# A fused macaron block on one core: the feed-forward's residual moved from VectorE to TensorE and ScalarE, its block scales made once, its layer norm halves joined by GpSimd

## The reference

```python
def fp4_quant_dequant(x):            # blocks of 16 along the last dim
    scale = jnp.maximum(jnp.max(jnp.abs(xb), axis=-1, keepdims=True) / 6.0, 1e-12)
    xn = xb / scale
    idx = jnp.searchsorted(_MID, jnp.abs(xn))
    return (_GRID[idx] * jnp.sign(xn) * scale).reshape(shape)

def _L1_ffn_ref(x, w_gate, w_up, w_down):        # 128 -> 352 -> 128
    gate = fp4_linear(x, w_gate)                 # both operands through fp4_quant_dequant
    y = fp4_linear(x, w_up)
    h = jax.nn.silu(gate) * y
    return fp4_linear(h, w_down)

x = x + 0.5 * _L0_ffn_ref(_layernorm(x), ...)    # mixture of experts
x = x + _L0_attn_ref(_layernorm(x), ...)         # linear attention
x = x + 0.5 * _L0_ffn_ref(_layernorm(x), ...)
x = x + 0.5 * _L1_ffn_ref(_layernorm(x), ...)    # "ffn_a"
x = x + _L1_attn_ref(_layernorm(x), ...)
x = x + 0.5 * _L1_ffn_ref(_layernorm(x), ...)    # "ffn_b"
```

## Time and profile before

| | |
|---|---|
| median of 3 runs | 868.86 us |
| lowest and highest | 866.7 and 873.04 us |
| the profiled execution, its own time | 870.8 us |
| its span in the profile | 869.0 us |
| mean granted TensorE clock | 0.896 of full speed |
| PE, DVE, ACT, POOL busy | 81%, 78%, 54%, 19% of the span |
| DVE's products of gate and up (L1085) | 428.9 to 846.6 us, in both feed-forwards |

### The profile page before, as it was taken

The page is one execution under the profiler, slowest core; times in us unless marked ns, Lnnn a source line. Parts: engine busy times, 40 slices in busy tenths (PEclk is TensorE's granted clock), DMA queues, the critical chain, the costliest instruction groups (busy, mean ns, idle before and its releaser), DMA issues.

```text
span 869.0 us, 17382 instructions
## 1 busy us (share of the span) xinstructions
PE 703.0 (81%) x6018; PEld 533.8 (61%) x6018; DVE 676.8 (78%) x1671; ACT 466.8 (54%) x893; POOL 164.6 (19%) x323
## 2 busy tenths in 40 slices
PE   3999999798986999999585777468989865857774
PEld 2777776677775677776354665436686663546654
DVE  2888787375656578789799999649899956999995
ACT  3787777656460677777464455264323114644552
POOL 4001021645542100101111210022110001112100
PEclk9999999899999899999768788868999987687888
DMA  7000000000000000000000000000000000000000
GB/s 197 2 0 0 0 1 2 3 3 2 0 3 3 1 1 0 0 1 0 1 0 0 0 0 0 1 0 1 1 0 0 1 0 1 12 12 12 12 24 25
DMA packets 13454, 6.99 MB, mean 8 GB/s; under 512 B 1177, under 2 KB 13409, under 8 KB 13409
## 3 DMA queue, kind: packets, MB, share of 16 engines
q1 hardware_dynamic: 10464, 5.26, 2.3%
q10 hardware_dynamic: 2944, 1.12, 0.5%
HBM read 4.28 MB, written 2.10 MB: 7 GB/s over the span
## 4 chain that ended last, share of the span: by engine, by line
PE 60%; DVE 26%; issue 7%; ACT 3%; DMA 1%; POOL 1%; DVEq 0%; SPq 0%; POOLq 0%; ACTq 0%
PE ps L1171 53%; PE ps L1470 4%; DVE ffn_work L723 3%; DVE shared L998 2%; DVE ffn_work L728 2%; DVE picked L900 2%; PE ps L1483 2%; DVE hq L734 1%; DVE x_sb L819 1%; DVE xn L734 1%; ACT xn L435 1%; DVE ffn_work L717 1%; DVE fq_x_max L700 1%; DMA wraw<-ttn_out_proj_weight_dram 1%; DVE attT L906 1%
## 5 line engine op out<-in xcount | busy, mean ns | idle before, releaser
L1171 PEld LDWEIGHTS ps<-w_sb,sq_h 128*128 128x128 f32 x1024 | 131.9, 192 | 68.8 <-ACT sq_h L457 50.7
L819 DVE SCALAR_TENSOR_TENSOR x_sb<-ps,gates,x_sb 128x128 f32 (+1 forms) x512 | 147.8, 345 | 20.4 <-PE ps L1171 12.3
L294 POOL TENSOR_SCALAR vareps<-meanvar 128x4 f32<-128x4 f32 (+1 forms) x44 | 25.0, 568 | 606.4 <-DVEq L763 606.4
L1171 PE MATMUL ps<-w_sb,sq_h 128*128 128x128 f32 x1024 | 138.0, 278 | 0.9 <-ACT sq_h L457 0.9
L1171 PE MATMUL ps<-xnT,w_sb 128*128 128x512 f32 x256 | 135.4, 613 | 0.0
L453 ACT ACTIVATE relu_h<-ps 128x512 f32<-128x512 f32 x128 | 75.7, 591 | 57.6 <-PE ps L1171 57.3
L435 ACT ACTIVATE xn<-x_sb,shift,rstd 128x128 f32 (+1 forms) x192 | 79.8, 481 | 18.3 <-POOL shift L302 18.2
L457 ACT ACTIVATE sq_h<-relu_h 128x512 f32<-128x512 f32 x128 | 80.6, 630 | 4.0
L1483 PE MATMUL ps<-ident,xn 128*128 128x128 f32 x64 | 16.8, 414 | 70.8 <-DVE xn L734 70.8
L1171 PE MATMUL ps<-ident,shared 128*128 128x128 f32 x512 | 64.6, 290 | 10.3 <-DVE shared L998 10.3
L1171 PE MATMUL ps<-downT,hqT 128*128 128x128 f32 x384 | 71.2, 339 | 0.5 <-ACT hqT L631 0.5
(11 more groups left out here) (147 smaller groups left out, 1270.1 us busy)
## 6 DMA issues: line engine op xcount, KB each, us to landing
x_sb<-in_L_attn_x_dram SPq DMA_DIRECT2D x8, 256.0 KB, 6.4
out_dram<-x_sb SPq DMA_DIRECT2D x8, 256.0 KB, 2.3
w_sb<-in_L_ffn_w_all_dram ACTq DMA_DIRECT2D x2, 512.0 KB, 7.4
wraw<-in_L_attn_qkv_w_dram SPq DMA_DIRECT2D x1, 192.0 KB
wraw<-attn_in_proj_weight_dram SPq DMA_DIRECT2D x1, 192.0 KB
fraw<-in_L_ffn_w_down_dram SPq DMA_DIRECT2D x1, 176.0 KB, 3.5
fraw<-in_L_ffn_w_gate_dram SPq DMA_DIRECT2D x1, 128.0 KB, 4.0
fraw<-in_L_ffn_w_up_dram SPq DMA_DIRECT2D x1, 128.0 KB, 3.1
```

Of the source, the lines that this page charges most:

```text
L819: t = nc.vector.scalar_tensor_tensor(tile_b(i, j), bank(4 + e % 4, TPB, C)[:, j, :], gates[:, j, e:e + 1], tile_b(i, j), ALU.mult, ALU.add)
L1171: return nc.tensor.matmul(o, a, b, start=start, stop=stop, **kw)
```

## The change

Three things, in both feed-forwards.

**The residual.** DVE's `residual` is gone. PE multiplies `x_sb` of the group by the identity into bank 7 before the down products (`x_under`), these add on top (`start=False`), and ACT copies the bank back to `x_sb` (`x_out`). The factor 0.5 and the signs go into the weights when ACT copies them out, once.

**One scale a block.** `scales` with its two instructions is replaced by `nudged_scales` with one; the quotient and the product back use the same scale.

**The layer norm.** DVE no longer joins the two halves that the sums instruction leaves (`ln_moments` falls away for groups 2 to 7); POOL does that from the raw sums with ten small instructions in place of four (`ln_from_halves`). DVE takes the sums of group i+3 in the middle of body i, where they were those of group i+2 at its start.

```diff
+            def ln_from_halves(s, i, n):
+                half = stats[:, 0:n, :]
+                mean_sum, mean_gap, gap_sq, spread, var = [sums[:, k, 0:n] for k in range(5)]
+                base = 9 * (i - 2)
+                pool.wait_ge(s["stats_ready"], i - 1)
+                pool.sem_inc(s_passed_pool, 1)
+                k = step(0, nc.gpsimd.tensor_tensor(mean_gap, half[:, :, 1], half[:, :, 4], ALU.subtract))
+                k = step(k, nc.gpsimd.tensor_tensor(mean_sum, half[:, :, 1], half[:, :, 4], ALU.add))
+                k = step(k, nc.gpsimd.tensor_tensor(spread, half[:, :, 2], half[:, :, 5], ALU.add))
...
+                k = step(k, nc.gpsimd.tensor_tensor(rstd[:, 0:n], vareps[:, 0:n], minus_half[:, 0:n], ALU.pow))
@@ ACT
+                def x_out(i):
+                    act.wait_ge(s["down_done"], i * TPB + TPB)
+                    act.sem_inc(s_passed_act, 1)
+                    nc.scalar.activation(group_b(i), bank(7, TPB, C), ACT.Copy).then_inc(s["x_done"], 1)
@@ ACT body
                         act.wait_ge(s["tr_done"], i + 2)
                         normal(i + 2)
+                    if not (type(i) is int and i == 0):
+                        x_out(i - 1)
                     act.wait_ge(s["h_divided"], i + 1)
                     magnitude(fq_h[0], fq_h[1]).then_inc(s["h_sized"], 1)
@@ DVE
-                def residual(i):
-                    dve.wait_ge(s["down_done"], i * TPB + TPB)
-                    nc.vector.scalar_tensor_tensor(group_b(i), bank(7, TPB, C), 0.5, group_b(i),
-                                                   ALU.mult, ALU.add).then_inc(s["x_done"], 1)
+                def halves(i):
+                    for j in range(TPB):
+                        t = nc.vector.bn_stats(stats[:, j, :], tile_b(i, j))
+                    t.then_inc(s["stats_ready"], 1)
@@ DVE body
-                    if ahead:
-                        ln_stats(s, ch, i + 2, TPB, tile_b)
                     dve.wait_ge(s["up_ready"], i * TPB + TPB)
...
                     h4.largest()
-                    h4.scales()
-                    h4.inverse()
+                    h4.nudged_scales()
+                    h4.inverse(h4.sl)
                     h4.divide()
-                    if behind:
-                        residual(i - 1)
                     if ahead:
                         dve.wait_ge(s["xn_ready"], i + 3)
                         x4 = x_stream(i + 2)
                         x4.largest()
...
                         x4.divide()
+                    if further:
+                        halves(i + 3)
                     h4.snap()
@@ PE
+                def x_under(i):
+                    if not (type(i) is int and i == 0):
+                        pe.wait_ge(s["x_done"], i)
+                    mm(bank(7, TPB, C), ident[:, :], group_b(i), start=True, stop=False, skip_group_check=True)
@@ PE body
                         x_transposes(i + 2)
+                    x_under(i)
                     pe.wait_ge(s["hq_ready"], i + 1)
                     hidden_transposes(i, 0)
```

More of the change, by code:

```diff
@@ L115, in macaron @@
         shift = sb("shift", [P, 8])
+        sums = sb("sums", [P, 6, TPB])
         xn = sb("xn", [P, 8, C])
@@ L631, in hidden_T, with body @@
                     nc.scalar.activation(hqT[:, j % 2, :, :], bank(5 + j % 2, 3, P), ACT.Copy).then_inc(s["hT_ready"], 1)
-                def body(i, ahead, last):
+                def x_out(i):
+                    act.wait_ge(s["down_done"], i * TPB + TPB)
+                    act.sem_inc(s_passed_act, 1)
+                    nc.scalar.activation(group_b(i), bank(7, TPB, C), ACT.Copy).then_inc(s["x_done"], 1)
+                def body(i, ahead, last, further=False):
                     if ahead:
@@ L661, in ffn @@
                 evac_xnT(s, 1)
-                with act.Fori(0, GROUPS - 2) as i:
-                    body(i, True, False)
+                body(0, True, False, True)
+                with act.Fori(1, GROUPS - 3) as i:
+                    body(i, True, False, True)
+                body(GROUPS - 3, True, False)
                 body(GROUPS - 2, False, False)
                 body(GROUPS - 1, False, True)
+                x_out(GROUPS - 1)
             moe(S["moe_a"], S["linatt"], True)
@@ L1077, in x_alone, with body @@
                     x4.rescale()
-                def body(i, ahead, behind):
-                    if ahead:
-                        ln_stats(s, ch, i + 2, TPB, tile_b)
+                def halves(i):
+                    for j in range(TPB):
+                        t = nc.vector.bn_stats(stats[:, j, :], tile_b(i, j))
+                    t.then_inc(s["stats_ready"], 1)
+                def body(i, ahead, further):
                     dve.wait_ge(s["up_ready"], i * TPB + TPB)
@@ L1116, in ffn @@
                 x_alone(0)
+                dve.wait_ge(s["xn_ready"], 2)
+                halves(2)
                 x_alone(1)
                 pre = ch.k
[L1119 to L1123, removed]
+                with dve.Fori(0, GROUPS - 3) as i:
+                    ch.start(i * PER["ffn"] + pre)
                     body(i, True, True)
                     assert ch.k == PER["ffn"], ("ffn", ch.k)
-                pre += (GROUPS - 3) * PER["ffn"]
-                ch.start(pre)
-                body(GROUPS - 2, False, True)
-                body(GROUPS - 1, False, True)
+                ch.start((GROUPS - 3) * PER["ffn"] + pre)
+                body(GROUPS - 3, True, False)
+                body(GROUPS - 2, False, False)
+                body(GROUPS - 1, False, False)
                 if first:
@@ L1475, in down @@
                     for k in range(3):
[L1476 removed]
+                        t = mm(bank(7, TPB, C)[:, j, :], hqT[:, j % 2, k, :], downT[:, k, :], start=False, stop=k == 2,
+                               skip_group_check=True)
                     t.then_inc(s["down_done"], 1)
@@ L1501, in ffn @@
                 x_transposes(1)
-                with pe.Fori(0, GROUPS - 2) as i:
+                body(0, True, False)
+                with pe.Fori(1, GROUPS - 2) as i:
                     body(i, True, False)
```

57 lines of the change are left out of this document (42 added, 15 removed).

## The result

The changed kernel takes 880.06 us (median of 4 runs, 879.4 to 883.55) against 869.64 us (4 runs, 866.7 to 873.04): ratio 1.0131, 95% interval 1.0092 to 1.0169. It is slower by 1.3%. 886.9 was forecast, range 876 to 898: the direction and the range hold, the loss is 10.4 us where 18 were expected.

What follows compares the result with a forecast made beforehand. DVE and the chain X, PE, ACT's hidden copies, ACT's normalised x were taken to bound the kernel together. Two feed-forwards (+16.0) and POOL (+2.0) on 870.8 made 888.8; 1.9 lower for the median, 886.9 us, range 876 to 898.

Steps and rivals of the forecast that it cites:

- The bound: DVE and a chain through PE and ACT end together; 2.6 us less DVE work a body gains nothing.
- X: The moment at which DVE ends the last product on xn; one body, 17.10 us, runs between two of them.
- first stretch: From X to DVE's start on the largest of the next xn blocks: 8.35 us, not below about 8.3.
- The sums: Four sums instructions of group i+3, behind the quotient of xn, stand exposed on DVE: 0.82 us with the hand-over.
- second stretch: From DVE's start on the largest xn block to the next X: 8.75 us, forecast to become 9.47.
- The identity product: On PE ahead of the hidden transposes, 1.70 us at low clock; delays the chain 0.55 us, bounds 0.1 and 2.4.
- The copy in body 6: ACT's copy of bank 7 precedes the hidden magnitude there, so DVE waits: 2.0 us later.
- Body 7: Last body of the feed-forward: magnitude waits for DVE's quotient anyway, identity product fits PE's wait; put at -0.13 us.
- POOL: Its ten small instructions may hold DVE: 0.2 us a body, +2.0 in all.
- the count of five slips a body: Between sums and X, a small POOL instruction slips in between DVE's two-operand operations some five times, 0.04 us each.
- The sum: +8.0 us for one feed-forward, +16.0 for two, +2.0 for POOL: in all +18.
- (b): Rival: PE mostly finds the clock rising early, delay 0.15, POOL's part 0; 5.6 a feed-forward, 880 us; chance 0.22.

Runs made afterwards that it cites:

- e6: Changed kernel with identity product before xn transposes, sums before the xn wait, magnitude before bank 7's copy, ACT normalising between hidden copies: 847.57 us, ratio 0.9747.
- e2: Changed kernel with DVE taking the sums of group i+3 before it waits for ACT's xn: 872.93 us, ratio to before 1.002.
- e1: Changed kernel with PE's identity product moved ahead of the transposes of xn, inside PE's pause: 867.49 us, ratio to before 0.9949.
- e3: Changed kernel with its residual part undone (residual back on DVE, no identity product or ACT copy): 871.8 us, ratio to before 1.0019.
- e7: Kernel e3 plus a useless 128x512 product in PE's pause, ahead of the transposes of xn: 861.27 us, ratio to before 0.9906.
- e5: Changed kernel with identity product before xn transposes, sums before the xn wait, and body 6's magnitude before the copy: 856.37 us, ratio 0.9835.

## Why the prediction was right, and what was mis-sized

**The bound.** Right. The chain X, PE, hidden copies, normalised x holds the first stretch; DVE's 2.6 us less work became 2.3 to 3.5 us of waiting for L475, as stated. e6 shows it from the other side: with the normalised x taken out of that place, and the product and the sums moved, the wait is gone and the stretch is DVE's 6.5.

**The sums.** Right in size and place: second stretch 9.48 measured, 9.47 worked out. Removing that exposure (e2) gives 7.1 us.

**The identity product.** The place was right (e1), and so was its duration, 1.71 against 1.70. The delay that follows was mis-sized: the mean first stretch grew by 0.17 us, not by 0.55. This is the term of the sum that failed most, 3.8 of the 18 us forecast. The step took the middle between a rise of the clock as late as before (delay 0.9 to 1.0) and one at 3.7 us (0.1 to 0.2). Measured are distances of 3.0 to 5.7 us from the restart, and in four of the ten bodies a restart that still finds the clock up and then has it low for 3.4 us. The first stretches run from 8.15 to 9.33. The long ones are the first case; the short ones are below the second, whose least delay, 0.1, would have made 8.45: in five of the ten the stretch is shorter than that, with the product in it. The working had taken for granted that each restart finds the clock low.

**The copy in body 6.** The mechanism was right and the sum had a slip. 0.55 + 1.36 and a hand-over is the distance from the copy's start to the rounding step; the kernel before already had 0.60 of that between the residual and the rounding step, as the same passage says, and it was not taken off. With it off, 2.0 becomes 1.4, and 1.4 is measured (14.52 against 13.15 from product to product). The idle time is 3.75 where "some 4" was said. Body 7 hid the slip: put at -0.13, it cost 0.4, and its clock rose 4.7 us after the restart at 559.75 where it had risen 3.7 after the one at 555.26. Together it is 1.7 a feed-forward (from X of body 5 to the end of the last copy or residual 34.3 against 32.6), where 1.9 had been summed. That these two agree is luck.

**POOL.** Forecast +2.0, bounds 0 and 11. Measured next to nothing: one rounding step a body is 0.03 us longer, and the second stretch is 9.48 where 9.47 was worked out without POOL. The step that failed is the count of five slips a body; there is one. The contention is there, but nearly all of it falls on POOL.

**The sum.** For one feed-forward, from the first product of gate and up to the end: 133.41 us before and 139.49 after in the first, 133.39 and 139.25 in the second; +6.1 and +5.9, where 8.0 and 1.0 for POOL were forecast. That is 3.0 less than the 9.0 forecast: 1.9 for the delay, 1.0 for POOL and 0.1 for bodies 6 and 7. Together +11.9. The span grew by 8.4, so 3.5 of it were met by shorter times outside: the first product of gate and up comes 1.1 us earlier, and the stretch between the two feed-forwards, which holds the attention and the start of the second one, is 2.4 us shorter. Such shifts come without an edit: in the ten traces DVE starts on the first feed-forward at 411.6 to 416.9 us, with the same instructions ahead of it but for the factors of the weights, and e3 and e7, whose instructions between the feed-forwards are the same, have 170.3 and 167.1 us there. How much of the 3.5 would last stays open; the medians give 10.4. The range holds with either.

**The rivals.** (b), the kind clock, at 880, is the case that came about, with a chance of 0.22 against 0.43 for the forecast. It named the mechanism, and its delay of 0.15 is near the 0.17 measured; its sum of 5.6 a feed-forward is near the 6.0 of the trace. The reason given against it, that the product does not shorten the pause, only says that the clock does not stay up for good. It overlooked that the restart itself moves against the clock: in e3, which has no product, it falls 1.4 us further into the low spell and the rise is nearer by as much.

## What to carry to other kernels

Before work is taken off an engine that seems full, look for every chain that ends at the same moment as its work: here three did, within 0.2 us, and freeing DVE alone gained nothing. The gains came as the chain through PE and ACT was shortened (e1, e5), and DVE's wait went only when the order on ACT was changed too (e6). Work that is moved is free only if it goes to a place where its engine waits: the same product cost 12.6 us more ahead of the hidden transposes than in PE's pause, the same sums 7.1 us more behind the wait than in front of it. Where PE pauses in every body, as here, its clock is a part of the chain: it hid most of a loss of 0.7 us a body (e3) and gave 10 us for a filler (e7). Compare the distance from restart to rise before reading a small difference as the price of an edit. And when an added step is priced, take off what already stood in its place: in body 6 that was 0.60 us.

## What the runs showed of the hardware that was not expected

- A useless 128x512 product in a pause of PE made a kernel 10.5 us faster (e7 against e3). In the traces 6.6 of it lie in the feed-forwards, with the clock low for 3.4 us a body in place of 6.8.
- POOL's small instructions beside DVE operations with two SBUF operands stretch from 0.20 to 1.41 us, and DVE's lose 0.03 us at most, whereas a large one, the bias in the kernel before, held DVE's L998 for 2.2 us. The Trainium skill, "GPSIMD Engine Reference", section Specifications, states the contention; these runs agree with it, and in them POOL bears it where its operands are small.
- The two parts of the change cost 0.2% and 0.5% alone and 1.3% together.
